# One wait of an attention and mixture-of-experts kernel: results of experts given out with at most two transfers under way in place of four

## The reference

```
x = x + attn_block(layernorm(x))      # causal attention, 16 heads of 8, rotary; then a dense
                                      # MLP 128 -> 512 -> 128 with gelu
x = x + moe_block(layernorm(x)):
    x1 = layernorm(x + attention(x) + bo)          # not causal
    p  = softmax(x1 @ Wg + bg)                     # 8 experts
    topk_p, topk_i = top_k(p, 2);  topk_p /= sum(topk_p)
    y_e = gelu(x1 @ W1[e] + b1[e]) @ W2[e] + b2[e] # 128 -> 512 -> 128
    out = layernorm(x1 + sum of topk_p * y_e over the two chosen experts)
```

## Time and profile before

| | us |
|---|---|
| median of three runs | 1774.73 |
| lowest, highest | 1770.65, 1775.59 |
| profiled execution | 1774.01 |
| its span | 1771.9 |

### The profile page before, as it was taken

How to read it: one execution, slowest core, us unless ns; L and a number is a source line. 1 busy time by engine, 2 the same in 40 slices (tenths; PEclk the granted TensorE clock), 3 DMA queues, 4 the chain that set the end, 5 groups by cost and what they waited for, 6 DMA issues and landing times.

```text
span 1771.9 us, 39180 instructions
## 1 busy us (share of the span) xinstructions
PE 1460.8 (82%) x15249; PEld 669.7 (38%) x15249; DVE 1266.9 (71%) x1972; ACT 1169.5 (66%) x2373; POOL 378.5 (21%) x418
## 2 busy tenths in 40 slices
PE   5679999989998788569999998999889978964980
PEld 3324444444443455212222223222322236863870
DVE  6787777778785266599999998999789842510254
ACT  7537677777687655319999997898779964421341
POOL 5300000000000355200000002000213321556264
PEclk9869899999899999759999999999989989986995
DMA  4513422121112343400001020002001314642763
GB/s 143 187 54 119 143 82 89 40 85 57 63 40 69 91 121 116 151 19 31 32 32 38 33 69 32 31 34 76 24 34 54 106 34 136 189 159 91 233 206 108
DMA packets 132777, 152.94 MB, mean 86 GB/s; under 512 B 13744, under 2 KB 107824, under 8 KB 132336
## 3 DMA queue, kind: packets, MB, share of 16 engines
q1 hardware_dynamic: 122480, 123.43, 22.4%
q0 software_dynamic: 10112, 27.01, 4.1%
HBM read 90.90 MB, written 63.46 MB: 87 GB/s over the span
## 4 chain that ended last, share of the span: by engine, by line
PE 19%; DVE 19%; DMA 12%; issue 9%; ACT 4%; POOL 2%; SPq 1%; another core or an unknown queue 0%; ACTq 0%; POOLq 0%; DVEq 0%
DVE row_max L629 14%; DMA sorted_in<-v_all,slots 7%; PE bank L596 6%; PE banks L572 4%; PE banks L540 2%; PE banks L1434 2%; PE banks L1444 2%; ACT probs L683 2%; DMA qk_parts<-parts 1%; DMA probs<-x_mid_d 1%; DVE probs L1801 1%; POOL sorted_in L1221 1%; DMA pair_out<-k_work,pairs 1%; PE banks L1377 0%
## 5 line engine op out<-in xcount | busy, mean ns | idle before, releaser
L629 DVE TENSOR_REDUCE row_max<-banks 128x2 f32<-128x1024 f32 (+3 forms) x896 | 938.7, 1101 | 137.4 <-PE banks L546 74.4
L683 ACT ACTIVATE probs<-banks 128x512 f32<-128x512 f32 (+3 forms) x1792 | 879.7, 551 | 191.5 <-PE banks L572 91.0
L596 PE MATMUL bank<-probs,v_ones 128*32 128x256 f32 (+3 forms) x7168 | 537.2, 377 | 20.0 <-ACT o_sums L694 16.8
L572 PE MATMUL banks<-q_work,k_work 51*128 51x512 bf16 (+3 forms) x1792 | 385.7, 373 | 51.1 <-DMA q_work<-max_T 33.5
L540 PE MATMUL banks<-k_work,q_work 48*128 48x512 bf16 (+3 forms) x1792 | 366.0, 381 | 74.4 <-DVE row_max L629 59.5
L572 PEld LDWEIGHTS banks<-q_work,k_work 51*128 51x128 bf16 x1792 | 102.4, 93 | 420.8 <-ACT probs L683 319.8
L721 POOL DMA_DIRECT2D heads_out<-o_sums x64 | 35.6, 556 | 1011.3 <-ACT o_sums L694 1011.3
L596 PEld LDWEIGHTS bank<-probs,v_ones 128*32 128x32 f32 x7168 | 147.3, 109 | 256.3 <-ACT probs L683 184.2
L2041 ACT ACTIVATE rope<-banks,expert 128x256 f32<-128x256 f32 x184 | 72.1, 474 | 169.4 <-PE banks L1434 124.5
L540 PEld LDWEIGHTS banks<-k_work,q_work 48*128 48x128 bf16 x1792 | 95.0, 96 | 140.5 <-DVE row_max L629 108.8
L1434 PE MATMUL banks<-rope,expert 128*128 128x256 f32 x368 | 93.7, 400 | 34.3 <-issue 27.0
(11 more groups left out here) (209 smaller groups left out, 1162.1 us busy)
## 6 DMA issues: line engine op xcount, KB each, us to landing
expert<-expert_rows SPq DMA_DIRECT2D x46, 578.0 KB
qk_parts<-parts SPq DMA_DIRECT2D x64, 256.0 KB, 3.3
heads_out<-o_sums POOLq DMA_DIRECT2D x64, 256.0 KB, 4.4
q_work<-qk_parts SPq DMA_DIRECT2D x64, 128.0 KB
k_work<-qk_parts SPq DMA_DIRECT2D x64, 128.0 KB
sorted_in<-zeros SPq DMA_DIRECT2D x4, 1472.0 KB, 12.4
parts<-sorted_in SPq DMA_DIRECT2D x22, 256.0 KB
q_work<-qk_parts SPq DMA_DIRECT2D x64, 64.0 KB
```

What stands on the lines that cost most here:

```text
L572: last = pe.matmul(to[par][:, 0:G - c0], k[r:r + M1, pair, kt * P:(kt + 1) * P], q[r:r + M1, pair, qh * G + c0:(qh + 1) * G], start=True, ...
L596: last = pe.matmul(bank[7][32 * j:32 * j + 32, c0 + part * w:c0 + (part + 1) * w], v_ones[i % QB][:, kt, j, :], prob_slots[:, (e + j) % RI ...
L629: dve.tensor_reduce(row_max[:, qt, 2 * pair:2 * pair + 2, kh], self.buf_of("chunk", g, c)[:, :, 0:width], AX.X, ALU.max).then_inc(s["chunk ...
L683: act.activation(prob_slots[:, e % RING, 0:width], banks46[:, e % EXP_BANKS, 0:width], ACT.Exp, scale=SCALE).then_inc(s["exps"], 1)
```

## The change

A constant is added and used in the one place where give-outs wait:

```diff
 ON_WAY = (1, 2)
+GIVEN_ON_WAY = 2
...
             def give_out(m):
...
                 for side in range(SIDES):
                     at = SIDES * j + side
                     n = given_number(section, at)
-                    landed(n - LANES)
+                    landed(n - GIVEN_ON_WAY)
```

## The result

The change made the kernel slower: 1783.83 us (median of five runs, 1783.15 to 1788.21) against 1774.74 for the kernel before in the same session (1770.65 to 1777.97), a ratio of 1.0063 with a 95% interval of 1.0037 to 1.0088. The forecast was 1766, faster. The time lies in the range, but on the side to which I had given 0.20. The profiled execution took 1783.83 with a span of 1781.7.

What follows compares the result with a forecast made beforehand. Pool's last give-out was taken to bound the end. Give-outs and roots summed to 138.9 us, ending at 1725.4 against 1737.8: 12.4 us less, 3 given back, so 1775 - 9 = 1766 us; own range 1754 to 1776, stated range 1753 to 1785.

Steps and rivals of the forecast that it cites:

- The stall goes under a limit of two: Section 0's backlog: Pool's enforced pauses let PE's late handovers through; the reserve is 26.4 us of PE standing still.
- The first rival: The stall stays: one late handover locks it while Pool runs at full pace in quiet; +6, 1781 us; chance 0.27.
- The first 12 give-outs at 0: Give-outs before section 0's backlog: at most 6.1 us later, mostly covered by 2.66 us of Pool idling, so taken as 0.
- The traffic price of 2.135 us taken from the scatters: Give-outs while expert weights flow: 2.135 us each in place of 1.262, so 0.87 more, as section 1's scatters showed.
- In 78 us at 2.135 Pool issues 36.5. Remaining: 37.5, quiet: Last 80 give-outs: after 6 quiet ones, 36.5 under traffic lasting 78 us, the remaining 37.5 in quiet, 47.3 us.
- some 20 blocks: PE's blocks for which weights flow: 20 x 3.73 = 74.6 us, taken as 78 since DVE's combining lies in the later ones.
- The quiet pace of 1.262: Give-outs where DMA is quiet: Pool keeps its full pace of 1.262 us each under a limit of two.
- The 3 us given back: Taken off the 12.4 us gain for waits, such as 2.41 us before 1694.58, that will not all vanish.
- The fixed tail of 35.3 us: From Pool's last give-out at 1736.58 to the end: 35.3 us, so the end moves one for one with it.
- The Trainium skill's fixed 2 us for a transfer: Fixed DMA cost of about 2 us; by it alone two under way would always do, and the sum would be nothing.

Runs made afterwards that it cites:

- The experiment of 17 pauses: Kernel before (limit four) with one small Pool operation ahead of each of the last 17 blocks of section 0: 1759.46 us, ratio 0.9878 to the kernel before.
- with the roots earlier: Changed kernel (limit two) with section 0's four tail_roots after blocks 2, 5, 8, 11 of section 1, not 6, 9, 12, 15: 1784.74 us, ratio 1.0047.
- after: The changed kernel, limit of two in both sections against four in the kernel before: 1783.83 us, ratio 1.0063.
- halved loads: Changed kernel (limit two) with expert loads cut to half their bytes, except the first into each buffer: 1769.86 us, ratio 0.9969 to the kernel before.
- The swapped kernel: Changed kernel (limit two) with side 0 waiting first for the landing, then for y, in place of y first: 1777.91 us, ratio 1.0003 to the kernel before.

## Why the prediction was wrong

*The stall goes under a limit of two*: right, and for the reason given, the pauses, as far as it went (pauses or the slower pace that they bring). The experiment of 17 pauses carries it, since there the limit stays at four. The first rival (one late handover locks it) did not happen.

*The first 12 give-outs at 0*: too low. From the third on they wait up to 2.25, 1.40, 1.55 and 3.35 us for landings, and the backlog starts 2.35 us later, of which 0.7 us was there before the first give-out.

*The traffic price of 2.135 us taken from the scatters*: right for section 0. Forecast for its 34: 7.6 + 28 x 2.135 = 67.4 us, measured 66.8.

*"In 78 us at 2.135 Pool issues 36.5. Remaining: 37.5, quiet"*: **this step failed.** It let the traffic end 78 us after it began. Measured, SP issues its last load of an expert at 1708.20, and the traffic price is paid until about 1713; 34.9 us of PE's waits for Pool fall into that time. For the 24 give-outs from 1655.57 to 1712.59 the sum had 8.5 at 2.135 and 15.5 at 1.262, 37.7 us; measured 52.5, **14.8 too few**. I had listed who waits behind Pool, and priced none of it. But the experiments show that those waits are not themselves most of the loss: with the roots earlier they were 11.8 us shorter and Pool needed nearly the same time, and with the limit back at four in section 1 it is fast although the first wait stays. The loss is Pool's own pace, 2.19 us on average over these 24, because there a landing is not back within two steps of 1.262 (by the lanes' semaphores 2.1 to 7.2 us). The kernel before did this stretch at a limit of four, near its free pace, and there it had been the bound.

What the 78 us left out is what else moves. These are transfers in after from 1655.6 to 1712.6 (how many, KB each, median us from issue to landing):

```profile
DMA packets 11180, 10.94 MB, mean 192 GB/s; under 512 B 809, under 2 KB 9769, under 8 KB 11177
...
expert<-expert_rows SPq DMA_DIRECT2D x8, 578.0 KB
probs<-pair_out SPq DMA_DIRECT2D x8, 256.0 KB, 5.6
probs<-x_mid_d SPq DMA_DIRECT2D x4, 256.0 KB, 6.7
...
out_x<-probs SPq DMA_DIRECT2D x2, 256.0 KB, 4.3
```

The 21 loads of experts in the traffic (13 before 1655.6, 8 here) are the "some 20 blocks" of the sum. The combining of section 0 brings 14 transfers of 256 KB more, and the sum had 3.4 us for it. Pool's loss against its free pace goes with what moved: 21.0 us for 10.5 MB in the scatters of the earlier trace rows, 23.9 us for 12.1 MB in section 0's part of after, 22.2 us for 10.9 MB here, 21.6 us for 11.1 MB with the roots earlier, each 1.9 to 2.0 us per MB. My estimate from that: the kernel before moved 23.7 MB from 1590 to 1724 (134 us at 177 GB/s, the last column of the row below), which makes 47 us, where the sum had 36.5 x 0.87 = 31.9. The difference, some 15 us, is about the 14.8 that were missing. It is no constant: with halved loads it was 2.2 and then 1.5 us per MB, with the waits swapped 1.8 and 1.7 (3.4 of the 14.8 us went with the swap). No run leaves the combining's transfers out, so their share is argued and not shown.

```profile
1590.00:1724.00 134.00, 98.55 (x614) 90.22 (x614) 38.59 (x126) 42.03 (x108) 69.30 (x75) 0.84 0.57 177
```

*The quiet pace of 1.262*: wrong for a limit of two, taken from scatters, which have one wait; a side 0 has two. For the last 22 give-outs 27.8 us stood in the sum, measured 33.5: **5.7 too few**. The order of the waits is 2.6 us of it (the swapped kernel took 30.9). The other 3.1 are waits and longer issues such as the kernel before has there too (30.4 us for its last 22), and for such the 3 us had been given back. The row that would have told of the order is in the list of instructions: two waits beside each side 0, with the landing's on the instruction of its own. The swapped kernel shows it, and with 8.5 us over all 80 it alone brings back the 0.6%.

The sum from there: forecast end 1725.4, + 2.35 + (66.8 - 67.4) + 14.8 + 5.7 = 1747.6; measured 1746.59 + 0.96 = 1747.55. The 3 us given back are not in this sum.

*The fixed tail of 35.3 us*: right, 35.1.

*The Trainium skill's fixed 2 us for a transfer* (DMA: Bandwidth & Descriptors, anatomy of a DMA): the quiet landing of 2.25 us agrees. As a constant it does not hold: under traffic, from 1655 to 1713 in after, landings of 64 KB took 2.1 to 7.2 us, and the waits for them up to 5.09.

Not settled: what holds PE's handovers back while Pool issues without a pause. The runs show when they are held and what prevents it, not by which path. The semaphores' own records narrow it down. In calm stretches PE's semaphore rises 0.01 to 0.02 us after the end of PE's product (as the profile gives ends). In the stall that of `down` rose at 1605.76 for a product that ended at 1598.72, and at 1633.89 for one that ended at 1610.11, and DVE started 0.02 us after each rise. So it was PE's increment that came late, by 7.0 and 23.8 us, not DVE that was slow to see it. DVE's handovers to PE were not late in the same stretch: PE started 0.15 us after DVE's end at 1606.20 and 0.11 us after its end at 1630.72. Of the traffic price, the halved weights gave 6.0 of the (66.8 - 42.9 =) 23.9 us of section 0; the rest (rows, results, the other half of the weights) was not taken apart.

## What to carry to other kernels

A limit on transfers under way is paid wherever the issuing engine is the bound, and earned only where its pauses free somebody else: price it stretch by stretch, and set it for each stretch. When a stall goes, the work behind it moves into the limited engine's traffic. Count then what has to move, all of it, and not how long the other engine's own work would last: here the loss of the limited engine went with the megabytes, whether they came in 40 us or in 57. Where an instruction has two waits, let it carry the one that comes last itself.

## What was not expected of the hardware

- ACT and DVE waited 4 to 30 us for handovers of products that PE had ended long before, while Pool issued indirect DMAs every 1.262 us. One operation of 1.04 us after every second DMA was enough to prevent it; six in 34 were not. Halved weight traffic changed little in it (18.63 and 6.42 us against 20.72 and 5.69). PE's semaphore itself rose 7.0 and 23.8 us after PE's product had ended, in place of 0.01 to 0.02.
- With two under way a landing of 64 KB took 2.25 us in quiet and up to 7.2 us with some 190 GB/s beside it, and Pool lost 1.9 to 2.0 us per MB moved, in the scatters as in the give-outs of after.
- From a landing to the next Pool DMA 0.28 us pass if the DMA waits for it itself, and 0.70 us if a wait instruction does and the DMA has a second wait, already fulfilled.
